# Attention on one Trainium2 core: every fourth score tile from bf16 parts, in the array shape of the value products, and a dealt copy of the keys

## The chip, the cores and the metric

The kernel runs on one core of a Trainium2 chip. The metric is device time of one execution, in microseconds (us). Engines are named as in the profile: PE (matmuls), PEld (PE's weight loads), DVE (vector), ACT (scalar), POOL (GpSimd), SP (the engine that issues most transfers).

## The reference

Two layers, each attention and a feed-forward part. The change concerns the attention of the first, over 4096 tokens of 256 features, 16 heads of 16:

```
q, k, v = split_heads(x @ Wq.T + bq), split_heads(x @ Wk.T + bk), split_heads(x @ Wv.T + bv)
scores = einsum('hbnd,hbmd->hbnm', k, q) / 16
attn   = softmax(scores, axis=-1)                 # over the 4096 m
out    = einsum('hbnm,hbmd->hbnd', attn, v)       # then @ Wo.T + bo
```

`x` is the normalised input. Everything is float32 at the interface.

## The kernel before, in words

The stages run one after the other: weights are turned (`setup_phase`), projections (`qkv0_phase`), attention (`attention_phase`), the first feed-forward part, and the second layer. Each engine runs its own program; waits are on semaphores counted.

**Projections.** Eight blocks of 512 tokens. PE makes queries and keys feature by feature, in four slices c = 0 to 3 of 128 features (0, 1 queries, 2, 3 keys). ACT writes the high part (fp32r) of each, DVE the low part (`low`, L450); SP stores both parts to the scratch tensors QS and KS (L348). DVE also writes the values into `V_all`. POOL does nothing.

**Attention.** Heads go in pairs, eight of them, and a pair's 4096 key positions in eight blocks of 512: 64 steps. `QST` holds the pair's queries and `KST` (four slots) the blocks' keys as stacks of 16-row parts (high, high, low against high, low, high), so that one matmul of 48 rows makes a product of split numbers. Head e of the pair has rows 64e and up, so the two heads' matmuls use different row halves of PE's array. For every block two kinds of product are made:

- A tiles (`unit_a`, L624): keys as weights, every fourth key for each of four groups, 512 queries streamed. DVE takes the maxima over queries (L719), one reduction of 128 x 1024 for the two heads of a pair of A tiles. After 32 of them `neg` (L726) is the negative maximum of every key; POOL cuts it into parts (L749, L751) and SP writes them as two more rows of `KST` (`load_shift`, L587).
- Score tiles (`unit_s`, L636): 128 queries as weights, 50 rows, 512 keys streamed, into one of three PSUM banks `SB`. ACT takes the exponential (L696) into `PR`. A score tile waits until ACT has read the bank's tile before it, three earlier (`s_free`).

The A tiles run one block ahead and LEAD = 8 chunks more. The values (`values`, L646) are products of 128 rows and 32 columns: four of them stand side by side in PE's array, each with its own 32 columns, one for each head and each of two chunks, accumulating over all chunks in one bank `PV` of 128 x 512. In fp32 each is two matmul instructions. PE's order per two chunks of 128 queries: score head 0, A pair, score head 1, the same again, then four values products. At a step's end ACT copies `PV` to `OS` (L707), POOL moves the odd chunks' groups beside the even ones by two transfers (L763), adds them (L766), and stores numerators and denominators (L773). Keys of a block are loaded by six transfers three steps ahead (L572), queries of the next pair by six at a pair's first step. Each engine's attention program is a loop whose body holds 16 steps, turned four times.

## Time and profile before

| | us |
|---|---|
| time, median of 3 runs | 5075.87 (5071.74 to 5075.96) |
| the profiled execution: its time | 5077.41 |
| its span in the profile | 5075.5 |
| PE busy in the span | 4705.6 |
| DVE busy | 3645.4 |
| ACT busy | 3173.7 |
| POOL busy | 394.2 |

The span is what the profile covers; the profiled execution took 1.9 us more than it, and 1.5 us more than the median. A busy PE is not PE at its peak: its matmuls are pipelined and overlap in the records, so the distance of their starts counts.

### The profile page before, as it was taken

The page shows a single profiled execution, that of the slowest core. Times are in us where ns is not written, and L with a number is a line of the kernel's source. Part 1 is how long each engine was busy: PE and PEld are TensorE (multiplying, and loading weights), DVE is VectorE, ACT ScalarE, POOL GpSimd, SP SyncE. Part 2 cuts the span into 40 slices and gives each one's busy share as a digit, 9 for nine tenths or more (in the row PEclk, how much of TensorE's full clock was granted, in tenths as well). Part 3 has the DMA queues.
Part 4 walks back from the last instruction along what each step waited for, and adds up shares of the span by engine and source line. Part 5 has one row for each costly group of instructions (what it writes and reads, how often), then busy time and mean ns, then how long its engine had stood idle before and what let it go on. Part 6 is the DMA issues. An engine that isn't in the chain of part 4 may idle for free. (4 is left out here: it accounts for less than half of the span.)

```text
span 5075.5 us, 80926 instructions
## 1 busy us (share of the span) xinstructions
PE 4705.6 (93%) x24956; PEld 2773.9 (55%) x24956; DVE 3645.4 (72%) x3695; ACT 3173.7 (63%) x5605; POOL 394.2 (8%) x866
## 2 busy tenths in 40 slices
PE   6699999999999999999999959999885399999999
PEld 4344444444444444444444437777654177777777
DVE  4789999899998999998999965565455444444444
ACT  3178778788887787787878744444473344444444
POOL 0001111111111111111111100000000000000000
PEclk8699999999999999999999979999997699999999
DMA  4310100100101001001010020000001400000000
GB/s 146 96 16 12 26 12 12 22 13 13 25 12 24 12 12 25 13 13 23 12 25 12 13 81 25 33 25 17 23 21 46 114 6 11 12 12 12 12 12 13
DMA packets 145888, 135.28 MB, mean 27 GB/s; under 512 B 83360, under 2 KB 102192, under 8 KB 144720
## 3 DMA queue, kind: packets, MB, share of 16 engines
q1 hardware_dynamic: 133296, 114.48, 9.1%
q0 software_dynamic: 12288, 16.80, 1.6%
q8 instruction: 185, 3.03, 0.3%
q14 instruction: 119, 0.97, 0.1%
HBM read 80.33 MB, written 41.94 MB: 24 GB/s over the span
## 5 line engine op out<-in xcount | busy, mean ns | idle before, releaser
L719 DVE TENSOR_REDUCE PM<-A 128x2 f32<-128x1024 f32 x2090 | 2460.9, 1221 | 292.9 <-PE A L624 292.9
L696 ACT ACTIVATE PR<-SB 128x512 f32<-128x512 f32 x4100 | 2118.2, 605 | 548.0 <-PE SB L636 539.7
L636 PE MATMUL SB<-KST,QST 50*128 50x512 f32 x4100 | 1508.6, 449 | 20.3 <-issue 8.4
L636 PEld LDWEIGHTS SB<-KST,QST 50*128 50x128 f32 x4100 | 699.9, 191 | 1186.7 <-ACT PR L696 1158.5
L624 PE MATMUL A<-QST,KST 48*128 48x512 f32 x4180 | 1273.1, 484 | 37.5 <-DMA QST<-QS 24.7
L646 PE MATMUL PV<-PR,VH 128*32 128x512 f32 x8192 | 1098.8, 609 | 0.0
L624 PEld LDWEIGHTS A<-QST,KST 48*128 48x128 f32 x4180 | 764.3, 306 | 106.9 <-DVE PM L719 43.0
L1860 DVE TENSOR_TENSOR m_h_lo<-m_h_full,m_h_hi 128x512 fp32r<-128x512 f32 x320 | 221.7, 693 | 285.3 <-ACT m_h_hi L1765 285.0
L1765 ACT CAST m_h_hi<-m_h_full 128x512 fp32r<-128x512 f32 x320 | 198.5, 620 | 245.5 <-DVE m_h_full L1857 243.4
L1857 DVE TENSOR_TENSOR m_h_full<-m_h_full,m_c 128x512 f32<-128x512 f32 x256 | 175.3, 685 | 235.2 <-ACT m_h_full L1759 204.8
L646 PEld LDWEIGHTS PV<-PR,VH 128*32 128x32 f32 x8192 | 161.5, 108 | 252.5 <-issue 163.4
L1759 ACT ACTIVATE m_h_full<-m_h,m_b 128x512 f32<-128x512 f32 x256 | 175.8, 687 | 195.1 <-PE m_h L58 194.4
L1071 DVE SCALAR_TENSOR_TENSOR chosen<-gate_out,h_ps 128x512 f32<-128x512 f32 x128 | 87.2, 681 | 181.1 <-PE h_ps L58 181.1
L1010 ACT ACTIVATE h_full<-chosen,b 128x512 f32<-128x512 f32 x128 | 92.4, 722 | 198.0 <-DVE chosen L1071 197.2
L56 PE MATMUL m_h<-ln_hi,moe_w_hi 128*128 128x512 f32 x512 | 208.7, 408 | 0.0
L57 PE MATMUL m_h<-ln_lo,moe_w_hi 128*128 128x512 f32 x512 | 202.8, 396 | 0.0
L56 PE MATMUL m_y<-m_h_hi,moe_w_hi 128*128 128x512 f32 x512 | 201.9, 394 | 0.0
L58 PE MATMUL m_h<-ln_hi,moe_w_lo 128*128 128x512 f32 x512 | 201.8, 394 | 0.0
L58 PE MATMUL m_y<-m_h_hi,moe_w_lo 128*128 128x512 f32 x512 | 201.5, 394 | 0.0
L57 PE MATMUL m_y<-m_h_lo,moe_w_hi 128*128 128x512 f32 x512 | 200.3, 391 | 0.0
L1080 DVE TENSOR_TENSOR h_lo<-h_full,h_hi 128x512 fp32r<-128x512 f32 x192 | 131.3, 684 | 71.6 <-ACT h_hi L1012 71.3
L1656 POOL CAST pick_pair<-pick 128x128 fp32r<-128x128 f32 x256 | 81.7, 319 | 1003.9 <-PE m_c L1678 1002.0
(283 smaller groups left out, 5187.4 us busy)
## 6 DMA issues: line engine op xcount, KB each, us to landing
QST<-QS SPq DMA_DIRECT2D x54, 256.0 KB, 8.4
KST<-KS SPq DMA_DIRECT2D x402, 32.0 KB, 1.8
QS<-parts SPq DMA_DIRECT2D x16, 512.0 KB, 2.8
KS<-parts SPq DMA_DIRECT2D x16, 512.0 KB, 2.8
OG<-OS POOLq DMA_DIRECT2D x128, 64.0 KB, 1.9
m_x<-X3T SPq DMA_DIRECT2D x16, 512.0 KB, 3.7
KST<-NM SPq DMA_DIRECT2D x260, 2.0 KB, 2.0
x_tok<-in_L_attn_x SPq DMA_DIRECT2D x8, 512.0 KB, 4.7
```

The lines of the kernel that those rows point to most:

```text
L56: nc.tensor.matmul(out, w[0], x[0], start=first, stop=False)
L57: nc.tensor.matmul(out, w[0], x[1], start=False, stop=False)
L58: return nc.tensor.matmul(out, w[1], x[0], start=False, stop=last)
L624: return nc.tensor.matmul(A[:, u % 2 * 2 + e, :], keys, QST[rows, slot, j * TB:(j + 1) * TB], start=True, stop=True)
L636: nc.tensor.matmul(SB[:, s_bank(v), :], QST[rows, slot, c * P:(c + 1) * P], KST[rows, nb % K_SLOTS, :], start=True, stop=True).then_inc(s_ ...
L646: mm = nc.tensor.matmul(PV[at:at + 2 * HD, :], VH[:, slot, e, c, :], PR[:, (2 * c + e) % P_SLOTS, :], start=(k == 0), stop=(k == PVS - 1))
L696: nc.scalar.activation(PR[:, v % P_SLOTS, :], SB[:, s_bank(v), :], ACT.Exp, scale=SCALE).then_inc(s_free, 1)
L719: nc.vector.tensor_reduce(PM[:, par, :, i, j:j + 1], A[:, u % 2 * 2:u % 2 * 2 + 2, :], AX.X, ALU.max).then_inc(a_free, 1)
L1759: nc.scalar.activation(h_full[:, c % RING, :], h_ps[:, c % 2, :], ACT.Silu, bias=bias).then_inc(full_ready, 1)
L1765: nc.scalar.copy(h[0][:, c % RING, :], h_full[:, c % RING, :]).then_inc(hi_ready, 1)
L1857: nc.vector.tensor_tensor(h_full[:, c % RING, :], h_full[:, c % RING, :], c_ps[:, c % 2, :], ALU.mult).then_inc(kept_ready, 1)
L1860: nc.vector.tensor_tensor(h[1][:, c % RING, :], h_full[:, c % RING, :], h[0][:, c % RING, :].bitcast(F32), ALU.subtract).then_inc(lo_ready, 1)
```

## The change

- Heads are paired (p, p + 8) in place of (2p, 2p + 1), so that head 1 of a pair lies in the features 128 and up.
- The score tile of head 1 and every odd chunk, one of four, is made by `unit_fine`: four matmuls of 99 rows and 32 columns, 512 keys streamed, side by side in the array. Its operands `QF` and `KF` are bf16, three parts of each number in six products of 16 rows, and three rows for the shift.
- The values are taken per chunk: four products, for two heads and two halves of 256 keys, into `PV[:, 0:256]`. `PV` then holds finished sums: POOL's two transfers and addition go, eight stores take their place. There are four values products more per two chunks, each of half the columns. The fine tile stands between the values of two chunks.
- PE's order per two chunks: A pair, score, score, score, A pair (its two halves in the other order), values, fine tile, values. LEAD is 10.
- A dealt copy of the keys, `KAD` in memory and `KA` on chip, holds each group of 128 keys of A's weights contiguously.
- The projections' new POOL program makes the dealt copy and the three bf16 parts of queries (features 128 and up, odd chunks) and keys; SP stores them after the block's other stores.
- Per block SP loads keys by 18 transfers in place of six, per pair queries by 12 in place of six, and the shift by seven in place of four.

```diff
@@ qkv0_phase, SP, per block
+                    for k in range(KC):
+                        sp.wait_ge(dealt_ready, count(((i + 2) * KC + (k + 1)) * PARTS))
+                        alone(sp, passed)
+                        sp.dma_start(d["KAD"].rearrange("j (k p) n -> p k j n", p=P)[:, k, :, ds(i, TB)],
+                                     dealt[slot][:, k, :, :].bitcast(F32)).then_inc(dealt_stored[slot], 16)
+                    for n, c in enumerate((1, 3)):
+                        sp.wait_ge(fine_ready, count(i * 2 * FINE + (n + 1) * FINE))
+                        alone(sp, passed)
+                        dst, cols = (d["QFD"], OB) if c == 1 else (d["KFD"], TB)
+                        sp.dma_start(dst.rearrange("j p n -> p j n")[:, :, ds(i, cols)],
+                                     fine[slot][c][:, :, :]).then_inc(fine_stored[slot], 16)
@@ qkv0_phase, POOL (new)
+                def fine_parts(half, i, slot, n, c):
...
+                    nc.gpsimd.tensor_tensor(of(whole), of(parts[slot][:, c, 0, :].bitcast(F32)),
+                                            of(parts[slot][:, c, 1, :].bitcast(F32)), ALU.add).then_inc(summed, 1)
...
+                    for j in range(FINE):
+                        nc.gpsimd.tensor_copy(part(j), of(left)).then_inc(fine_ready, 1)
+                        if j < FINE - 1:
+                            pool.wait_ge(fine_ready, count(k * FINE + (j + 1)))
+                            nc.gpsimd.tensor_tensor(of(rest[j]), of(left), part(j), ALU.subtract).then_inc(rest_ready, 1)
...
+                def deal(half, i, slot, c):
...
+                    for j in range(PARTS):
+                        nc.gpsimd.tensor_copy(dealt[slot][:, c - 2, j, :].bitcast(F32).rearrange("p (i q) -> p i q", i=TT),
+                                              parts[slot][:, c, j, :].bitcast(F32).rearrange("p (q i) -> p i q", i=TT)
+                                              ).then_inc(dealt_ready, 1)
+
+                def blocks(half, i, slot, following):
+                    fine_parts(half, i, slot, 0, 1)
+                    deal(half, i, slot, 2)
+                    deal(half, i, slot, 3)
+                    fine_parts(half, i, slot, 1, 3)
@@ attention_phase, SP
                 def load_k(pair, nb):
...
+                    load_stack(KA[:, nb % K_SLOTS, :], "KAD", K_PARTS, pair, cols, ready)
+                    load_stack(KST[:, nb % K_SLOTS, :], "KS", K_PARTS, pair, cols, ready)
+                    load_fine(KF[:, nb % K_SLOTS, :], "KFD", FINE_K, pair, cols, ready)
@@ load_shift
+                    sp.wait_ge(neg_fine, count((b + 1) * FINE))
+                    for j in range(FINE):
+                        row = FINE_STACK + j
+                        sp.dma_start(KF[row:row + 1, nb % K_SLOTS, :], NF[:, nb % 2, j, :], allow_slow_non_contiguous=True
+                                     ).then_inc(shift_loaded[nb % 2], 16)
@@ attention_phase, PE
-                    keys = KST[rows, nb % K_SLOTS, :].rearrange("r (p i) -> r i p", i=TT)[:, i, :]
+                    keys = KA[rows, nb % K_SLOTS, i * P:(i + 1) * P]
...
+                def unit_fine(t, c, nb, slot):
+                    v = 2 * c + 1
+                    pe.wait_ge(s_free, count(t * EXPS + (s_before(v) + 1 + S_BANKS)))
+                    for r in range(4):
+                        at = c // 2 * P + r * 2 * HD
+                        mm = nc.tensor.matmul(SB[r * 2 * HD:(r + 1) * 2 * HD, s_bank(v), :],
+                                              QF[0:FINE_ROWS, slot, at:at + 2 * HD],
+                                              KF[0:FINE_ROWS, nb % K_SLOTS, :], start=True, stop=True)
+                    mm.then_inc(s_done, 1)
+
+                def values(t, c, slot):
+                    if c == 0:
                         pe.wait_ge(pv_read, count(t))
...
+                    pe.wait_ge(s_free, count(t * EXPS + (2 * c + 2 + S_BANKS)))
+                    for e in range(2):
+                        for b in range(2):
+                            at = HALF * e + 2 * HD * b
+                            mm = nc.tensor.matmul(PV[at:at + 2 * HD, 0:HB], VH[:, slot, e, c, :],
+                                                  PR[:, (2 * c + e) % P_SLOTS, b * HB:(b + 1) * HB],
+                                                  start=(c == 0), stop=(c == MC - 1))
                     mm.then_inc(p_free, 1)
...
+                        units_a(t + ahead, u, a_nb, a_slot)
                         unit_s(s_t, q % MC, 0, s_nb, s_slot)
-                        units_a(t + ahead, u, a_nb, 1 - hp if past else hp)
                         unit_s(s_t, q % MC, 1, s_nb, s_slot)
...
+                        unit_s(s_t, q % MC + 1, 0, s_nb, s_slot)
+                        units_a(t + ahead, u + 1, a_nb, a_slot)
...
+                        values(t, q - 2, hp)
+                        unit_fine(s_t, q % MC + 1, s_nb, s_slot)
+                        values(t, q - 1, hp)
@@ attention_phase, ACT
-                    nc.scalar.copy(OS[:, nb % 2, :], PV[:, :]).then_inc(pv_read, 1)
+                    nc.scalar.copy(OS[:, nb % 2, :], PV[:, 0:HB]).then_inc(pv_read, 1)
@@ attention_phase, DVE, at the start
+                    nc.vector.memset(QF[:, s, :], 1.0).then_inc(rows_set, 1)
                     nc.vector.memset(QST[:, s, :].bitcast(F32), 1.0).then_inc(rows_set, 1)
@@ attention_phase, POOL, shift_parts
+                    left = neg[:, par, TT:2 * TT]
+                    for j in range(FINE):
...
+                        nc.gpsimd.tensor_copy(NF[:, par, j, :], left).then_inc(neg_fine, 1)
+                        if j < FINE - 1:
+                            pool.wait_ge(neg_fine, count(b * FINE + (j + 1)))
+                            nc.gpsimd.tensor_tensor(neg_rest[j][:, :], left, NF[:, par, j, :],
+                                                    ALU.subtract).then_inc(neg_left, 1)
...
@@ attention_phase, POOL, step
-                    for e in range(2):
-                        pool.dma_start(OG[HALF * e:HALF * e + 2 * HD, :],
-                                       OS[HALF * e + 2 * HD:HALF * (e + 1), nb % 2, :]).then_inc(groups_moved, 16)
-                    pool.wait_ge(groups_moved, (t + 1) * 32)
-                    nc.gpsimd.tensor_tensor(O2[0:P - 2 * HD, :], OS[0:P - 2 * HD, nb % 2, :], OG[0:P - 2 * HD, :],
-                                            ALU.add).then_inc(os_free, 1)
...
+                        for b in range(2):
+                            for j, name in enumerate(("NUM", "DEN")):
+                                at = HALF * e + 2 * HD * b + HD * j
+                                pool.dma_start(d[name][bass.ds(pair * HD + e * P, HD),
+                                                       nb * TB + b * HB:nb * TB + (b + 1) * HB],
+                                               OS[at:at + HD, nb % 2, :]).then_inc(o_stored, 16)
```

## Rows read from the trace of the kernel before

**Rows 1.** The page, busy time of each engine over the span.
```profile
PE 4705.6 (93%) x24956; PEld 2773.9 (55%) x24956; DVE 3645.4 (72%) x3695; ACT 3173.7 (63%) x5605; POOL 394.2 (8%) x866
```
**Rows 2.** ACT's copy by line: duration min/median/max in ns, first and last start in us.
```profile
L707 ACT COPY OS<-PV x64: 585/587/588, 296.2 to 2962.3; 128x512 f32<-128x512 f32 x64
```
**Rows 3.** Timeline of two periods: start, length (us), engine, line; idle before in brackets.
```profile
1504.88 0.50 PE L636 MATMUL SB<-KST,QST 50*128 50x512 f32 x1
...
1504.88 0.73 PE L624 MATMUL A<-QST,KST 48*128 48x512 f32 x2
...
1505.34 0.51 PE L636 MATMUL SB<-KST,QST 50*128 50x512 f32 x2
1505.41 2.06 ACT L696 ACTIVATE PR<-SB 128x512 f32<-128x512 f32 x4 [0.55 <-PE SB L636]
...
1505.56 0.51 PE L624 MATMUL A<-QST,KST 48*128 48x512 f32 x2
1505.64 2.36 DVE L719 TENSOR_REDUCE PM<-A 128x2 f32<-128x1024 f32 x2 [0.24 <-PE A L624]
1506.06 0.18 PEld L636 LDWEIGHTS SB<-KST,QST 50*128 50x128 f32 x1 [0.30 <-ACT PR L696]
1506.06 0.49 PE L636 MATMUL SB<-KST,QST 50*128 50x512 f32 x1
...
1506.48 1.06 PE L646 MATMUL PV<-PR,VH 128*32 128x512 f32 x8
...
1507.48 0.50 PE L636 MATMUL SB<-KST,QST 50*128 50x512 f32 x1
...
1508.04 0.22 DVE L726 TENSOR_REDUCE neg<-PM 128x8 f32<-128x64 f32 x1
1508.05 0.31 PEld L624 LDWEIGHTS A<-QST,KST 48*128 48x128 f32 x2
...
1508.91 1.77 SPq L587 DMA_DIRECT2D KST<-NM  x3
...
1510.09 0.50 PE L636 MATMUL SB<-KST,QST 50*128 50x512 f32 x1
```
**Rows 4.** Timeline of PE in the last stage, fp32 between fp32r matmuls.
```profile
4086.46 1.88 PE L130 MATMUL m_turn<-m_x,ones 128*128 128x512 f32 x4
...
4088.41 0.40 PE L57 MATMUL m_h<-ln_lo,moe_w_hi 128*128 128x512 f32 x1
4088.64 0.40 PE L58 MATMUL m_h<-ln_hi,moe_w_lo 128*128 128x512 f32 x1
```
**Rows 5.** PE's sequencer by line: the values' wait, and the loop's end.
```profile
L642 PEldq ALU_OP  x64: 32/32/32, 294.6 to 2960.6; - x64
...
L556 PEldq ALU_OP  x4: 32/32/32, 923.5 to 2960.8; - x4
...
L556 PEldq COMPARE_BRANCH  x4: 83/3856/4046, 923.7 to 2960.8; - x4
```
**Rows 6.** Timeline at the projections' end and attention's start, DVE and SP's queue.
```profile
176.90 0.75 DVE L450 SCALAR_TENSOR_TENSOR parts<-qk_ps,qk_bias,parts 128x512 fp32r<-128x512 f32 x1 [0.88 <-ACT parts L421]
...
183.87 2.67 SPq L572 DMA_DIRECT2D KST<-KS  x6
...
188.30 2.62 SPq L572 DMA_DIRECT2D QST<-QS  x6
```
**Rows 7.** One block of the projections: busy us of each engine, clock, DMA share, GB/s.
```profile
140.00:157.00 17.00, 14.02 (x69) 10.30 (x68) 11.63 (x12) 6.32 (x9) 0.00 (x0) 1.00 0.46 170
```
**Rows 8.** POOL's copy of the values by line.
```profile
L743 POOL COPY VH<-V_all x16: 609/612/617, 186.4 to 2302.0; 128x512 f32 x12, 128x512 f32<-128x512 f32 x4
```
**Rows 9.** A's weight loads by line.
```profile
L624 PEld LDWEIGHTS A<-QST,KST x4180: 304/306/338, 203.6 to 2960.0; 48*128 48x128 f32 x200
```
**Rows 10.** Timeline at attention's end, POOL.
```profile
2966.02 1.25 POOL L766 TENSOR_TENSOR O<-OS,OG 96x512 f32<-96x512 f32 x1 [1.51 <-DMA OG<-OS]
...
2972.39 0.48 POOL L773 DMA_DIRECT2D DEN<-O x1
```

More of the change, by code:

```diff
@@ L298 @@
 PARTS = 2
+FINE = 3
+OB = TB // 2
 def qkv0_phase(nc, d, K, V_all):
@@ L311, in qkv0_phase @@
         parts = [sb(f"parts{s}", [P, 4, PARTS, TB], F32R) for s in range(2)]
+        whole, rest = sb("whole", [P, TB], F32), [sb(f"rest{j}", [P, TB], F32) for j in range(2)]
+        fine = [{1: sb(f"fine_q{s}", [P, FINE, OB], BF16), 3: sb(f"fine_k{s}", [P, FINE, TB], BF16)} for s in range(2)]
+        dealt = [sb(f"dealt{s}", [P, KC, PARTS, TB], F32R) for s in range(2)]
         qk_bias = sb("qk_bias", [P, 4], F32)
@@ L321, in qkv0_phase @@
         qk_stored = [sem(f"qk_stored{s}") for s in range(2)]
+        fine_stored = [sem(f"fine_stored{s}") for s in range(2)]
+        summed, fine_ready, rest_ready, pool_passed = (sem(n) for n in ("summed", "fine_ready", "rest_ready", "pool_passed"))
+        dealt_ready, dealt_stored = sem("dealt_ready"), [sem(f"dealt_stored{s}") for s in range(2)]
         ln = LayerNorm("ln0", nc, sb, sem, K["ones"], [xT], xT_ready, ln_ps[:, 0, :], ln_ps[:, 1, :], 2)
@@ L444, in _, with of, part @@
                 overlapped(act, blocks)
+            @block.gpsimd
+            def _(pool):
+                def fine_parts(half, i, slot, n, c):
+                    def of(t):
+                        if c == 3:
+                            return t[:, :]
+                        return t[:, :].rearrange("p (a b m) -> p a b m", a=2, b=2)[:, :, 1, :]
+                    def part(j):
+                        return fine[slot][c][:, j, :] if c == 3 else fine[slot][c][:, j, :].rearrange(
+                            "p (a m) -> p a m", a=2)
+                    k = i * 2 + n
+                    pool.wait_ge(low_ready, count(i * 4 + (c + 1)))
+                    pool.wait_ge(fine_stored[slot], count(half * 32))
+                    pool.wait_ge(fine_ready, count(k * FINE))
+                    alone(pool, pool_passed)
+                    nc.gpsimd.tensor_tensor(of(whole), of(parts[slot][:, c, 0, :].bitcast(F32)),
+                                            of(parts[slot][:, c, 1, :].bitcast(F32)), ALU.add).then_inc(summed, 1)
+                    pool.wait_ge(summed, count(k + 1 + 4))
+                    alone(pool, pool_passed)
+                    left = whole
+                    for j in range(FINE):
[3 more added lines that the diff above has]
+                            nc.gpsimd.tensor_tensor(of(rest[j]), of(left), part(j), ALU.subtract).then_inc(rest_ready, 1)
+                            pool.wait_ge(rest_ready, count(k * (FINE - 1) + (j + 1)))
+                            alone(pool, pool_passed)
+                            left = rest[j]
+                def deal(half, i, slot, c):
+                    pool.wait_ge(low_ready, count(i * 4 + (c + 1)))
+                    pool.wait_ge(dealt_stored[slot], count(half * 32))
+                    alone(pool, pool_passed)
+                    for j in range(PARTS):
[7 more added lines that the diff above has]
+                    fine_parts(half, i, slot, 1, 3)
+                pool.sem_inc(summed, 4)
+                pool.sem_inc(dealt_ready, 2 * KC * PARTS)
+                overlapped(pool, blocks)
@@ L495 @@
 ROWS = STACK + PARTS
+FINE_K = (0, 0, 1, 0, 1, 2)
+FINE_Q = (0, 1, 0, 2, 1, 0)
+FINE_STACK = len(FINE_K) * HD
+FINE_ROWS = FINE_STACK + FINE
 HALF = P // 2
 SCALE = 1.0 / D ** 0.5
-LEAD = 8
+LEAD = 10
 EXPS = 2 * MC
-PVS = MC // 2
+HB = TB // 2
 S_BANKS = 3
@@ L534, in attention_phase @@
         NM = sb("NM", [P, 2, PARTS, 2 * TT], F32R)
-        OS = sb("OS", [P, 2, TB], F32)
-        OG = sb("OG", [P, TB], F32)
-        O2 = sb("O2", [P, TB], F32)
+        KA = sb("KA", [P, K_SLOTS, TB], F32R)
+        QF = sb("QF", [P, 2, T // 2], BF16)
+        KF = sb("KF", [P, K_SLOTS, TB], BF16)
+        NF = sb("NF", [P, 2, FINE, TT], BF16)
+        neg_rest = [sb(f"neg_rest{j}", [P, TT], F32) for j in range(FINE - 1)]
+        OS = sb("OS", [P, 2, HB], F32)
         A = ps("A", [P, 4, TB])
@@ L628, in units_a @@
                     pe.wait_ge(a_free, count(b * MC + (u + 1)))
-                    unit_a(u, 1, nb, slot)
-                    unit_a(u, 0, nb, slot).then_inc(a_done, 1)
+                    first = u % 2
+                    unit_a(u, first, nb, slot)
+                    unit_a(u, 1 - first, nb, slot).then_inc(a_done, 1)
                 def unit_s(t, c, e, nb, slot):
@@ L651, in step @@
                     t = number(two, hp, nb)
-                    for q in range(2, MC + 2):
+                    for q in range(2, MC + 2, 2):
                         ahead, u = divmod(q + LEAD, MC)
@@ L683, in _ @@
                 pe.wait_ge(shift_loaded[0], count(SHIFT))
-                for q in range(2):
-                    unit_s(0, q, 0, 0, 0)
-                    units_a(1, q + LEAD, 1, 0)
-                    unit_s(0, q, 1, 0, 0)
+                units_a(1, LEAD, 1, 0)
+                unit_s(0, 0, 0, 0, 0)
+                unit_s(0, 0, 1, 0, 0)
+                unit_s(0, 1, 0, 0, 0)
+                units_a(1, LEAD + 1, 1, 0)
+                unit_fine(0, 1, 0, 0)
                 in_steps(pe, step)
```

87 lines of the change are left out of this document (45 added, 42 removed).

## The prediction

> **What bounds the kernel.** I read the page first: PE 93%, DVE 72%, ACT 63% busy [rows 1]. Those are averages over five stages. The copy of the accumulated values happens once a step, 64 times from 296.2 to 2962.3 us [rows 2], so the attention stage is 63 steps in 2666.1 us, 42.32 us each, or 53% of the span. All of the change lies in it and in the projection stage before it.
>
> Next the timeline of one period, which is two chunks of 128 queries, sixteen to a step [rows 3]. The period is the distance of equal rows: 1504.88 to 1510.09 is two, so 2.605 us. The reader should see three things.
>
> *First*, PE's period has two sections. In the "stack" section (1504.88 to 1506.48, 1.60 us) four score tiles and two pairs of A tiles go, in the two row halves of the array, each half a queue of 512-column matmuls. In the values section (1506.48 to 1507.48, 1.00 us) eight matmul instructions go, four side by side, in two rounds.
>
> *Second*, the stack section holds a wait. Its first seven matmuls start at 1504.88 to about 1505.68 (the pair at 1505.56 ends at 1506.07 and each is 0.40 long). The last score tile starts only at 1506.06: its weight load stood 0.30 us behind ACT. That is the three-bank limit: tile 3 reuses the bank of tile 0, whose exponential starts at 1505.41 and takes 0.60. That row half had last started a matmul at 1505.56 and could have taken the next 0.23 later, so about 0.27 us of each period is PE waiting for an exponential.
>
> *Third*, the others have slack, but not much. ACT does its four in 2.06 and idles 0.55. DVE does its two reductions in 2.36 and idles 0.24, and the second A pair's weights (1508.05) come 0.05 after DVE's second reduction (1505.64 + 2.36 = 1508.00). So DVE stands right behind PE.
>
> **The stack section after.** One of four score tiles leaves, and it is the one that waited. Both row halves are now queues of four (A, score, score, A) and three. A half's queue advances by 0.23: in [rows 3] the tiles of one half start at 1504.88, 1505.22, 1505.45 and about 1505.68 (the first step also holds its exposed weight load, 0.10, which is 0.50 against 0.40 of duration). The last start is then at 0.81. From the last score's start to the values' start is 1506.48 - 1506.06 = 0.42; less its exposed weight load 0.10 it is 0.32. So the section is 0.81 + 0.32 = 1.13, 0.47 less than 1.60. The contiguous keys shorten the A weight load from 0.31 to at best the 0.18 of the score's [rows 3]; these loads lie beside running matmuls, so I give this nothing here (at best 0.1).
>
> **The values section after.** Before: two rounds, starting 1506.48 and 1506.95 (the group ends at 1507.54, a matmul of the second round is 0.59), so 0.46 a round. A 512-column fp32 matmul advances PE by 0.43 (four in 1.88 with 0.59 for the last [rows 4]), so a round costs 0.43 + 0.03, and the change of shape at the end 1.00 - 0.92 = 0.08. After: the same values work in four rounds of 256 columns, each 0.215 + 0.03 = 0.245, and one round for the fine tile, four bf16 matmuls of 512 columns. No bf16 matmul stands in the trace. Bounds for its round: 0.23, the spacing of single-pass matmuls [rows 4], and 0.46, the fp32 round of this shape. I take 0.25, since only its dtype is new and one pass of 512 columns has the former's length. Going from fp32 to another type costs nothing seen: the fp32 group's last start is 4087.75, and the second matmul behind it starts at 4088.41, which is 0.43 + 0.23 [rows 4]. Sum: 4 x 0.245 + 0.25 + 0.08 = 1.31.
>
> PE alone would then take 1.13 + 1.31 = 2.44, or 2.30 without the rounds' surplus over their columns.
>
> The rule that weighs against this change is in the Trainium skill, "TensorEngine Tiling (Array Packing)", Instruction Overhead: each matmul carries about 60 cycles. At 2.4 GHz that is 25 ns, as an estimate. By it the 20 instructions of the new values section cost 0.50 over their columns and the period is 2.30 + 0.50 = 2.80. The trace disagrees: the eight instructions of today's section cost 0.06 over their columns, not 0.20 [rows 3]; carried over by instruction that is 0.15, by round 0.14.
>
> Nor is the issuing of instructions the limit: between the values' wait (2960.6) and the loop's end (2960.8) PE's sequencer passes 16 instructions in 0.2 us [rows 5], and a period will have 54.
>
> **DVE's loop.** The first reduction can start when the first A pair is done. That pair now leads the section: 0.50 with an exposed load, 0.11 for the load of the second, 0.04 until DVE starts, 0.65 (before: 0.76, 1505.64 - 1504.88). Two reductions take 2.36, and the second A pair may load 0.05 later, at 3.06 from the start. It wants to load at 0.57 of the next period (1508.05 - 1507.48). If it comes x later, the section is x longer: P = 2.44 + x and P + 0.57 + x = 3.06, so x = 0.025 and P = 2.465. With PE at its lower bound (half rounds without the 0.03 and the fine round at 0.23: 2.30) the same two lines give 2.395. ACT, at four exponentials 0.49 apart, is hidden, and the fine tile's bank is free in time: exponential 0 ends near 1.36, the fine tile starts near 1.65.
>
> Saved: 2.605 - 2.465 = 0.14. Of 1024 periods I leave out 13, at the stage's start and after the three turns of its loop, where PE's branch takes 3.86 us [rows 5] and more code does not change that: 1011 x 0.14 = **-142 us**.
>
> **Once per step.** ACT's copy (0.59 [rows 2]) is halved and gets out of the exponentials' way; DVE's `neg` reduction (0.22), which fitted in the idle 0.24, loses part of its cover. I take 0 for both, bounds +-0.2 x 64 = +-13. POOL gets five more small operations (short like `neg`, 0.22, and as much waiting) and SP three more transfers (0.6 each, 1.77 for three [rows 3]) before the shift is in place: with two reductions, `neg` and seven transfers about 9 us, and the landing of the last. With LEAD 10 there are six periods, 14.7 us, from the block's last A pair to the next step's first score; with 8 there were five, 12.3, so it would be just enough. SP's 18 key loads per step at 0.45 each (six in 2.67 [rows 6]) are 8 us of 39, and at a pair's start 12 query loads add 5: both are hidden by the step.
>
> **Projection stage.** POOL was idle in it, and a block takes 17 us with the DMA engines 46% busy [rows 7]. Now POOL does, per block: three tensor-tensors of 512 and three of 256 columns, casts likewise, four dealing copies. From 1.25 for a tensor-tensor of 512 columns and 0.61 for a copy of 512 [rows 8, 10]: 3 x 1.25 + 3 x 0.73 + (4 + 3) x 0.61 + 3 x 0.4 + waits 1.5 = 13 us. That is under 17, so it is hidden except at the end: the last keys' part is ready at 177.65 [rows 6]; POOL then has about 10 us left, plus the store, where before only the store followed. **+10**. Collisions with DVE: none at best, at worst each of 16 large DVE operations behind a 1.25 operation, 20 us; I take **+5**. The Trainium skill, "SBUF — State Buffer", SBUF: two separate sides, has a VectorE operation with two SBUF inputs and a GpSimd operation that reads SBUF shut each other out for their whole length; by it the sum would have up to +20 there. No row shows it.
>
> **Start and end of attention.** SP's first keys are 18 loads, not 6: +5.3, of which 4.4 were spent waiting for the memset (183.87 to 188.30 [rows 6]), so the queries go out about 3.7 later; they are 12 transfers with a quarter more bytes, over the 13 us to the first A at 203.6 [rows 9]: +4. Two more A pairs before the first score: +2.3. Together **+10**. At the end the transfer of groups and the addition go: the stores ran from 2966.02 + 1.25 to 2972.9, now eight issues of 0.49 start at once [rows 10]: **-5**.
>
> **Sum:** -142 + 0 + 10 + 5 + 10 - 5 = -122. The profiled execution is 5077.4 us; the median 5075.9 is 1.5 lower. 5075.9 - 122 = **4954**.
>
> **Rivals.**
> *PE shorter (chance 0.27).* The shorter weight loads and cheap half rounds help, and DVE's loop decides: P = 2.395, -212, time 4884. For it: 0.31 against 0.18 of weight load. Against: those loads are covered.
> *A new wait in the loop (0.12).* The fine tile's exponential comes last and the next section's third score wants its bank; a period of 2.55: 1011 x 0.055 = -56, time 5040. For it: the chain before was one of this kind. Against: I find 0.2 us of slack.
> *POOL bounds the projection (0.08).* Strided dealing or collisions stretch 13 us over 17, say to 21: 8 x 4 = +32, time 4986.
> *Slower (0.06, and 0.01 for 25 ns on each of the 20 instructions, +0.195 x 1011 = +197, time 5250).* The four fine matmuls do not run side by side but one after the other, 0.92 instead of 0.25: P = 3.11, +510, time 5600. It decides from a fine round of 0.39 on (P 2.605). For it: four streams of the same rows in a new type are not in the trace. Against: fp32 ones run side by side.
> *The forecast (0.46).*
>
> So faster by over 0.2% (10 us, what a measurement here can tell) 0.92, within it 0.01, slower 0.07. The range holds the forecast, the first and third rivals and their bounds: 4865 to 5020.
>
> **What would show it.** Right: equal rows 2.40 to 2.50 apart; no weight load of a score behind ACT for 0.3; DVE with almost no idle; a values section near 1.3 with five rounds. Wrong: fine matmuls that start 0.23 apart; a section above 1.5; DVE idle while the period is above 2.5; the first A much after 225.

## The result, and the profile after the change

The changed kernel takes 4906.1 us (median of 4 runs, 4899.7 to 4913.5) where the kernel before takes 5075.9 (4 runs, 5071.7 to 5083.0): a ratio of 0.9665, with a 95% interval of 0.9647 to 0.9682. So it is 3.3% faster. The forecast was 4954 (4865 to 5020): the sign and the range are right, but the saving is 170 us and not 122. The profiled execution of the changed kernel took 4904.4, its span is 4902.7, against a span of 5075.5 before.

The page of the changed kernel, busy time of each engine, against [rows 1]:
```profile
PE 4503.7 (92%) x36227; PEld 2730.8 (56%) x36227; DVE 3647.4 (74%) x3699; ACT 3162.0 (64%) x5605; POOL 538.8 (11%) x1382
```
PE is busy for 202 us less, with 11271 more instructions. DVE and ACT do the same work as before.

**Where the 172.8 us of the span went.** Five marks cut it. The first and the last exponential stand in ACT's line (duration min/median/max in ns, then first and last start in us), of the changed kernel and then of the one before:
```profile
L814 ACT ACTIVATE PR<-SB x4100: 591/598/620, 284.6 to 2782.1; 128x512 f32<-128x512 f32 x196
```
```profile
L696 ACT ACTIVATE PR<-SB x4100: 592/606/633, 250.5 to 2961.4; 128x512 f32<-128x512 f32 x196
```
| stretch | before | after | difference | forecast |
|---|---|---|---|---|
| start to attention's first load (183.87, 208.34) | 183.9 | 208.3 | +24.5 | +15 |
| to the first exponential | 66.6 | 76.3 | +9.6 | +10 |
| first to last exponential | 2710.9 | 2497.5 | -213.4 | -142 |
| to the next stage's first load (2978.88, 2803.48) | 17.4 | 21.4 | +4.0 | -5 |
| the rest | 2096.6 | 2099.2 | +2.6 | 0 |

**The period.** The timeline of two periods of the changed kernel (start, length, engine, line), against [rows 3]:
```profile
1505.39 0.50 PE L724 MATMUL A<-QST,KA 48*128 48x512 f32 x2
...
1505.72 0.64 PE L737 MATMUL SB<-KST,QST 50*128 50x512 f32 x3
1505.86 0.18 PEld L737 LDWEIGHTS SB<-KST,QST 50*128 50x128 f32 x1 [0.18 <-ACT PR L814]
...
1505.95 0.65 PE L724 MATMUL A<-QST,KA 48*128 48x512 f32 x2
1506.15 2.06 ACT L814 ACTIVATE PR<-SB 128x512 f32<-128x512 f32 x4 [0.34 <-PE SB L737]
...
1506.54 0.64 PE L757 MATMUL PV<-PR,VH 128*32 128x256 f32 x8
...
1506.99 0.40 PE L745 MATMUL SB<-KF,QF 99*32 99x512 bf16 x4
...
1507.21 0.61 PE L757 MATMUL PV<-PR,VH 128*32 128x256 f32 x8
...
1507.76 0.49 PE L724 MATMUL A<-QST,KA 48*128 48x512 f32 x2
...
1510.16 0.49 PE L724 MATMUL A<-QST,KA 48*128 48x512 f32 x2
```
From 1505.39 to 1510.16 is two periods: 2.385 us each, where before had 2.605. The stack section (1505.39 to 1506.54) takes 1.15, the values section (1506.54 to 1507.76) 1.22. In the latter the first two rounds take 0.45, the fine tile's round 0.22, the last two with the change of shape 0.55. The only wait named is that of the third score's weights, 0.18 behind ACT. Over the whole stage the distance of the first exponentials of two steps has a median of 41.90 us before and 38.43 after, sixteen periods in each: 2.619 and 2.402.

**The end of the projections.** The last low part, POOL's work behind it, and attention's first load, against [rows 6]:
```profile
190.51 0.75 DVE L528 SCALAR_TENSOR_TENSOR parts<-qk_ps,qk_bias,parts 128x512 fp32r<-128x512 f32 x1 [1.09 <-ACT parts L448]
...
192.28 4.17 POOL L510 COPY dealt<-parts 128x512 f32<-128x512 f32 x4
...
196.41 1.26 POOL L491 TENSOR_TENSOR whole<-parts 128x512 f32<-128x512 f32 x1
...
201.86 0.61 POOL L497 CAST fine_k<-rest 128x512 bf16<-128x512 f32 x1 [0.17 <-POOL rest L500]
202.55 0.37 SPq L368 DMA_DIRECT2D KFD<-fine_k  x1
208.34 2.68 SPq L659 DMA_DIRECT2D KA<-KAD  x6
```
The last keys' low part is ready at 191.26, where it was ready at 177.65: 13.6 of the 24.5 us are lost before POOL's tail, and 10.9 in it.

One block of the projections after, beside [rows 7]: POOL is busy for 12.38 of 17 us, DMA 0.76.
```profile
140.00:157.00 17.00, 12.84 (x49) 8.34 (x47) 10.08 (x11) 6.23 (x8) 12.38 (x15) 0.90 0.76 275
```
The clock of a single block tells little: it is 0.90 here against 1.00 in [rows 7], but before the change it is 0.90 in the block ahead of that too (123 to 140 us). Over the whole stretch up to the last low part it is 0.95 before and 0.89 after:
```profile
52.00:178.00 126.00, 103.76 (x475) 76.15 (x474) 81.17 (x82) 44.78 (x58) 0.00 (x0) 0.95 0.49 174
```
```profile
52.00:191.00 139.00, 110.40 (x470) 79.19 (x470) 86.57 (x81) 45.45 (x59) 99.69 (x116) 0.89 0.65 232
```

### The profile page after: what moved, and what is told of

Read it like the earlier page. It is cut to its first block and busy times, and to the rows that moved or that the text cites. A ratio compares the mean times of both kernels' runs of the same rounds, so it can differ in the third digit from the quotient of the medians.

```text
span 4902.7 us, 107872 instructions
## 1 busy us (share of the span) xinstructions
PE 4503.7 (92%) x36227; PEld 2730.8 (56%) x36227; DVE 3647.4 (74%) x3699; ACT 3162.0 (64%) x5605; POOL 538.8 (11%) x1382
## 5 line engine op out<-in xcount | busy, mean ns | idle before, releaser
L757 PE MATMUL PV<-PR,VH 128*32 128x256 f32 x16384 | 1292.5, 386 | 2.4 <-issue 2.4
L724 PE MATMUL A<-QST,KA 48*128 48x512 f32 x4184 | 1193.2, 475 | 66.8 <-DMA QF<-QFD 41.7
L757 PEld LDWEIGHTS PV<-PR,VH 128*32 128x32 f32 x16384 | 432.9, 110 | 555.3 <-issue 367.8
L724 PEld LDWEIGHTS A<-QST,KA 48*128 48x128 f32 x4184 | 426.7, 187 | 524.0 <-issue 454.6
L737 PE MATMUL SB<-KST,QST 50*128 50x512 f32 x3075 | 687.6, 411 | 0.2
L737 PEld LDWEIGHTS SB<-KST,QST 50*128 50x128 f32 x3075 | 386.6, 186 | 207.8 <-ACT PR L814 204.8
L745 PE MATMUL SB<-KF,QF 99*32 99x512 bf16 x4100 | 415.7, 384 | 5.5 <-issue 4.3
L896 POOL DMA_DIRECT2D NUM<-OS x256 | 126.6, 494 | 864.2 <-ACT OS L825 721.0
```

Source lines behind the costliest of these rows:

```text
L724: return nc.tensor.matmul(A[:, u % 2 * 2 + e, :], keys, QST[rows, slot, j * TB:(j + 1) * TB], start=True, stop=True)
L737: nc.tensor.matmul(SB[:, s_bank(v), :], QST[rows, slot, c * P:(c + 1) * P], KST[rows, nb % K_SLOTS, :], start=True, stop=True).then_inc(s_ ...
L745: mm = nc.tensor.matmul(SB[r * 2 * HD:(r + 1) * 2 * HD, s_bank(v), :], QF[0:FINE_ROWS, slot, at:at + 2 * HD], KF[0:FINE_ROWS, nb % K_SLOTS ...
L757: mm = nc.tensor.matmul(PV[at:at + 2 * HD, 0:HB], VH[:, slot, e, c, :], PR[:, (2 * c + e) % P_SLOTS, b * HB:(b + 1) * HB], start=(c == 0), ...
```

## The experiments

Each is the changed kernel with one edit; the last has two together. Where no number of runs is given, the time is that of one run. The changed kernel's own runs lie within 14 us, so a difference of a few us in a single time tells nothing; such differences are read from the trace.

### The fine round between, ahead of or behind the values

The working had priced the fine tile at 0.25 and found 0.2 us of slack for its exponential. Moving its round tells whether PE or a chain through ACT sets the period.
```
-                        values(t, q - 2, hp)
                         unit_fine(s_t, q % MC + 1, s_nb, s_slot)
+                        values(t, q - 2, hp)
                         values(t, q - 1, hp)
```


> The fine tile stands ahead of both chunks' values, not between them; all else is as after the change. Theory (PE's two sections add up, and the fine tile is placed where its bank is free): it now waits for the exponential of the section's first score, which ends 1.36 us into the period where the values section begins at 1.15, so the period grows from 2.39 by about 0.25 to 2.63 and the time to about 5155. Rival (DVE's chain of reductions sets the period, the place of the tile is indifferent): period 2.39, time 4906.

Measured: 5111.6 us, periods 2.61 apart (the kernel before beside it: 5072.3). The timeline, weights and matmuls of the fine tile:
```profile
1505.54 0.10 PEld L745 LDWEIGHTS SB<-KF,QF 99*32 99x32 bf16 x4 [0.66 <-ACT PR L814]
1505.54 0.40 PE L745 MATMUL SB<-KF,QF 99*32 99x512 bf16 x4 [0.21 <-ACT PR L814]
```
The tile now waits for the exponential of the first score, which holds its bank, as the fourth score did in [rows 3]. The whole saving is gone: the same four matmuls are worth the saving only where a bank is free.
```
                         values(t, q - 2, hp)
-                        unit_fine(s_t, q % MC + 1, s_nb, s_slot)
                         values(t, q - 1, hp)
+                        unit_fine(s_t, q % MC + 1, s_nb, s_slot)
```


> The fine tile stands behind both chunks' values. Theory: its result is 0.43 us later, so its exponential ends about 3.05 after the period's start, and the third score of the next stack section waits for that bank: from 2.35 + x = P and P + 0.57 + x = 3.23 the period is 2.50, time about 5020, with a weight load of a score waiting about 0.3 us behind ACT. Rival (DVE's chain sets the period): 2.39, 4906.

Measured: 5146.6 us, periods 2.64 apart. This was a miss: I had reckoned 2.50. What is late is the *next* section's third score:
```profile
1505.98 0.18 PEld L737 LDWEIGHTS SB<-KST,QST 50*128 50x128 f32 x1 [0.46 <-ACT PR L814]
```
It wants the bank that the fine tile's exponential frees. In the changed kernel the same row shows 0.18 of waiting; here the fine round begins 0.33 before the section's end (1504.89 against 1505.22), its exponential at 1505.33. My figure had left out that the loop closes: when the section grows, the fine round moves back with it. So the middle place is the only one of the three that pays, and it is not free of ACT either (0.18).

### The tile back in the stack section, on the new kernel

```
                         unit_s(s_t, q % MC + 1, 0, s_nb, s_slot)
+                        unit_s(s_t, q % MC + 1, 1, s_nb, s_slot)
...
-                        unit_fine(s_t, q % MC + 1, s_nb, s_slot)
```


> The fourth score tile is made as before the change, one matmul of 50 rows in the stack section, last in it; everything else (order, values by chunk, dealt keys, projections) is as after. Theory (the gain is the fourth tile's place): the tile waits for exponential 0, which now ends 1.36 us into the period, starts at 1.41, the values section begins at 1.84 and lasts 1.00, so the period is 2.84 and the time about 5365, slower than before the change. Rival (order, dealt keys and values by chunk carry a share of the gain by themselves): period 2.6 or less, at most 5130.

Measured: 5348.7 us, periods 2.85 apart. With A leading the section and four half rounds, but the score in its old shape, the last score's weights wait for ACT, and the values stand behind them:
```profile
1507.11 0.18 PEld L737 LDWEIGHTS SB<-KST,QST 50*128 50x128 f32 x1 [0.66 <-ACT PR L814]
1507.11 0.50 PE L737 MATMUL SB<-KST,QST 50*128 50x512 f32 x1 [0.21 <-ACT PR L814]
1507.54 0.57 PEld L757 LDWEIGHTS PV<-PR,VH 128*32 128x32 f32 x13 [0.25 <-ACT PR L814]
```
(The prologue's one fine tile goes back too.) That is 0.47 us more than with the fine tile. So there is no gain without the tile's move: the order, the half rounds and the dealt keys without it make the kernel slower than before.

### The price of a fine round, and of the keys' layout

```
-                    for r in range(4):
+                    for r in range(8):
+                        r %= 4
```


> The fine tile is made twice (eight matmuls into the same bank, same result). Theory: one more round of 0.216 us in the values section; the 0.04 that PE loses to ACT and DVE is absorbed, so the period is 2.39 + 0.17 to 0.22, time 5080 to 5130. Rival (DVE sets the period and PE has slack): less than 0.05 more, under 4960.

Measured: 5085.0 us, periods 2.57 apart, 0.18 more. The eight matmuls and the next values:
```profile
1506.77 0.62 PE L746 MATMUL SB<-KF,QF 99*32 99x512 bf16 x8
...
1507.21 0.62 PE L758 MATMUL PV<-PR,VH 128*32 128x256 f32 x8
```
Two rounds take 0.44, so one takes 0.22: four bf16 matmuls of 512 columns do run side by side at the pace of one. That the period grows by less (0.18) is the wait behind ACT, which is used up.
```
-                    keys = KA[rows, nb % K_SLOTS, i * P:(i + 1) * P]
+                    keys = KST[rows, nb % K_SLOTS, :].rearrange("r (p i) -> r i p", i=TT)[:, i, :]
```


> The A tiles take their weights from the score keys with a stride of four, as before the change; the dealt copy is still made and loaded. Theory: the weight load grows from 0.18 to 0.31 us, and both pairs show it, the first because it opens the section, the second because it may only start when DVE's second reduction has ended: period 2.39 + 0.12 to 0.24, time 5030 to 5150. Rival (the prediction's: these loads lie beside running matmuls): 2.39, 4906.

Measured: 4996.0 us, periods 2.48 apart, 0.09 more, below the 0.12 to 0.24 expected (the second copy is still made and loaded).
```profile
1504.72 0.31 PEld L724 LDWEIGHTS A<-QST,KST 48*128 48x128 f32 x2 [0.41 <-issue]
1504.72 0.62 PE L724 MATMUL A<-QST,KST 48*128 48x512 f32 x2
```
The pair that leads the section is 0.62 long and not 0.50, since its load (0.31 and not 0.19) lies bare at the change of shape. So reading A's weights from the dealt copy is worth 90 us, with the fine tile in place; what making the copy costs in the projections is not in this number, and it is no share of the 170 that adds to the tile's own, since tile_in_stack loses over 440 us with the copy in place. I had given this 0, "at best 0.1": it is near the upper bound.

### Is DVE the bound of the loop?

This kernel reduces only half of A's columns, so each key's maximum is taken over half of the queries.
```
-                    nc.vector.tensor_reduce(PM[:, par, :, i, j:j + 1], A[:, u % 2 * 2:u % 2 * 2 + 2, :], AX.X,
+                    nc.vector.tensor_reduce(PM[:, par, :, i, j:j + 1], A[:, u % 2 * 2:u % 2 * 2 + 2, 0:TB // 2], AX.X,
```


> DVE takes the maxima over half of the columns only, so each reduction is about 0.7 us in place of 1.22; the maxima are then not the true ones. Theory: DVE costs the period only the 0.01 to 0.03 by which the second A pair's weights wait for it, so the period goes from 2.387 to 2.36 to 2.38 and the time to 4880 to 4900. Rival (DVE's chain sets the period): PE's own 2.30 or less, time under 4840.

Measured: 4882.0 us, but from the first to the last exponential 2494.4 against 2497.5, with the same period of 2.39. In the steady stretch from 300 to 850 us, the changed kernel, then this one (busy us of PE, PEld, DVE, ACT, POOL, clock, DMA share, GB/s):
```profile
300.00:850.00 550.00, 548.73 (x6156) 260.02 (x6152) 537.92 (x471) 474.86 (x926) 74.06 (x212) 1.00 0.12 22
```
```profile
300.00:850.00 550.00, 549.09 (x6178) 259.33 (x6171) 319.63 (x473) 475.78 (x929) 75.34 (x219) 1.00 0.12 22
```
DVE falls from 538 to 320 us and PE stays full. So the loop is at PE's length, with the third score's wait behind ACT in it, and DVE, busy for 98% of it, stands right behind without lengthening it. Of the 22 us by which the span is shorter, 15 came at the start, where DVE's reductions are the chain: the first exponential is at 269.2 and not 284.6.

### POOL in the projections

POOL's operations there are cut to an eighth of their columns; the rest of the dealt keys and bf16 parts is zero, set once.
```
-                            return t[:, :]
+                            return t[:, 0:TB // 8]
...
-                        nc.gpsimd.tensor_copy(dealt[slot][:, c - 2, j, :].bitcast(F32).rearrange("p (i q) -> p i q", i=TT),
+                        nc.gpsimd.tensor_copy(dealt[slot][:, c - 2, j, 0:TB // 8].bitcast(F32),
```


> In the projections POOL works on an eighth of the columns of each operation (the rest of the bf16 parts and of the dealt keys stays zero, so scores and maxima are not the true ones); the stores keep their size. Theory: the start of attention, first key load at 208.3 us against 183.9 before the change, is late by POOL's tail behind the last keys and by its collisions with DVE's operations; both shrink and the first key load comes at 184 to 190, time 4882 to 4888. Rival (the added stores, about 1.6 MB a block, hold the projections up): first key load still after 200.

Measured: 4883.4 us, attention's first load at 189.44 instead of 208.34, the exponentials' stretch unchanged at 2497.6. The last low part is ready at 178.65 (before 177.65), and POOL's tail with the store takes the rest. DVE's two large operations of the projections, after and in this kernel (count, busy us, mean ns, idle before):
```profile
L163 DVE TENSOR_TENSOR ln_lo<-ln_xc,ln_hi 128x1024 fp32r<-128x1024 f32 x8 | 14.7, 1834 | 4.3 <-ACT ln_hi L177 4.3
L157 DVE TENSOR_TENSOR ln_xc<-ln_xc,ln_sq 128x1024 f32<-128x1024 f32 x8 | 10.7, 1340 | 0.3
```
```profile
L163 DVE TENSOR_TENSOR ln_lo<-ln_xc,ln_hi 128x1024 fp32r<-128x1024 f32 x8 | 9.9, 1234 | 4.3 <-ACT ln_hi L177 4.3
L157 DVE TENSOR_TENSOR ln_xc<-ln_xc,ln_sq 128x1024 f32<-128x1024 f32 x8 | 9.8, 1226 | 0.3
```
18.9 of the 24.5 us go with POOL's columns: about 12.6 ahead of the last low part (13.6 less the 1.0 left here), the rest in the tail. POOL's width lengthens DVE's operations by 4.8 + 0.9 = 5.7 us in all. By the Trainium skill, "SBUF — State Buffer", SBUF: two separate sides, a VectorE operation with two SBUF inputs and a GpSimd operation that reads SBUF shut each other out, and the one that starts first keeps the other waiting for its whole length. The trace agrees. This is one block of the changed kernel:
```profile
160.65 1.10 POOL L510 COPY dealt<-parts 128x512 f32<-128x512 f32 x1 [2.10 <-DVE parts L528]
160.91 1.93 DVE L163 TENSOR_TENSOR ln_lo<-ln_xc,ln_hi 128x1024 fp32r<-128x1024 f32 x1 [0.45 <-ACT ln_hi L177]
161.68 2.14 POOL L510 COPY dealt<-parts 128x512 f32<-128x512 f32 x1
```
L163 starts 0.26 behind a dealing copy and ends 1.09 behind that copy's end, which leaves room for most of its own 1.22; the next copy takes 2.14 where their median is 1.12, and ends 0.98 behind L163. So it is in all seven blocks with a successor (1.91 to 1.93). It goes the other way in light_pool: there POOL's add of 64 columns starts 0.11 behind L163 and takes 1.30 in each of the seven, against 0.33 the one time that no L163 runs, and L163 keeps its 1.23.

The remaining 7 us of the 12.6 have no single row. No row has PE, ACT or DVE waiting for POOL there, though ACT's new program has such waits. SyncE's queue does wait for it ahead of the new stores, and ACT waits longer for PE's products. The clock up to the last low part is 0.89 in the changed kernel and 0.94 here:
```profile
52.00:179.00 127.00, 104.11 (x476) 76.19 (x475) 81.47 (x82) 45.34 (x59) 35.41 (x121) 0.94 0.75 263
```
As an estimate from these rows, 0.11 x 139 less 0.06 x 127 is 7.7 us of PE at its upper level. That would be enough, but no run parts the clock from the waits.

### The stores and the order of the first loads

```
                     load_shift(t + 1, (nb + 1) % NB)
+                    sp.wait_ge(pv_read, count(t + 1))
...
+                                sp.dma_start(d[name][bass.ds(pair * HD + e * P, HD),
...
-                    pool.wait_ge(pv_read, count(t + 1))
...
-                                pool.dma_start(d[name][bass.ds(pair * HD + e * P, HD),
```


> The eight stores of each step go out on SP's queue, behind the shift's transfers, instead of POOL's. Theory: the 10.5 us for which POOL drains at the stage's end belong to its own transfers and go; the period is unchanged; time about 4896. Rival (the drain has another cause): it stays, time 4906 or, if SP's queue makes the key loads late, more.

Measured: 4895.5 us. GpSimd's drain at the stage's end starts once its last eight stores have landed. Here it is in the changed kernel, in the one before, and in this one (duration in ns, start in us):
```profile
L652 POOLq DRAIN  x1: 10515/10515/10515, 2788.7 to 2788.7; - x1
```
```profile
L565 POOLq DRAIN  x1: 552/552/552, 2974.4 to 2974.4; - x1
```
```profile
L652 POOLq DRAIN  x1: 34/34/34, 2791.5 to 2791.5; - x1
```
In the changed kernel the stores have landed by 2788.7, 6.6 us behind the last exponential (before: 13.0), and the next stage's first load stands 14.8 us further on, 10.5 of which are the drain. With SyncE's stores that load is at 2795.51, 9.7 behind the last exponential (2785.8) and not 21.4. The drain is 10.515 us long in each of the nine kernels here whose GpSimd issues these eight stores.
```
-                load_k(0, 0)
+                load_stack(KA[:, 0, :], "KAD", K_PARTS, 0, slice(0, TB), first_a)
+                sp.wait_ge(rows_set, count(1))
+                load_stack(QST[:, 0, :], "QS", Q_PARTS, 0, slice(0, T), first_a)
...
-                load_q(0, 0)
+                load_stack(KST[:, 0, :], "KS", K_PARTS, 0, slice(0, TB), k_loaded[0])
...
+                pe.wait_ge(first_a, count(16 * 4 * len(K_PARTS)))
```


> Edit: at the start VectorE clears the queries' tile first, SyncE loads the first values-shaped keys, then the first queries, and only then the coarse keys and the fine ones, and TensorE's first A waits for the first two alone. Theory (the start of attention is a chain: last load, first A, DVE's reductions of the prologue, first exponential): the first A comes as many loads earlier as now stand ahead of it, three of about 2 us each, so the first reduction at about 229 us instead of 235.2, the first exponential 5 to 6 us earlier (279 instead of 284.6), the period 2.39 as before, and the time about 4900. Rival (the DMA transfers bound the start, whatever their order): first reduction at 233 or later and the time within 2 us of the changed kernel's 4906.

Measured: 4886.4 us. The first reduction starts 20.6 us behind the first load, as in the kernel before, where the changed kernel needs 26.8; the first exponential is at 277.7, 6.9 earlier:
```profile
207.60 2.68 SPq L660 DMA_DIRECT2D KA<-KAD  x6
...
212.04 2.62 SPq L660 DMA_DIRECT2D QST<-QS  x6
...
228.25 12.53 DVE L845 TENSOR_REDUCE PM<-A 128x2 f32<-128x1024 f32 x11 [7.68 <-PE A L731]
```
That is better than the 4900 expected, and only 6.9 of it is the edit's: of the 17.9 us by which the span is shorter, 9.4 lie between the first and the last exponential, most of them behind the turns of the loops.

Both edits together:

> Edit: the changed kernel with the other order of the first loads and with attention's stores issued by SyncE instead of GpSimd. Theory (the drain of GpSimd behind attention, 10.5 us of which about 10 lay on the path, and the loads ahead of the first A are terms of their own): their gains add, some 10 us from the stores and 5 to 6 from the start, so 4888 to 4892 us, a ratio to before of 0.963 to 0.964, with a period of 2.39. Rival (the earlier start only moves waiting to the keys of the second chunk, or SyncE's stores hold up the later loads of keys): 4895 or more.

Measured, in five runs, below the 4888 to 4892 expected: 4872.7 us (4869.6 to 4879.1), beside 5078.4 of the kernel before (9 runs on that chip): 0.9598, interval 0.9584 to 0.9611. So the version with both edits beats both kernels, the changed one by the ratio of the ratios, 0.9598 / 0.9665 = 0.993, some 34 us. Of these 6.8 lie ahead of the first exponential, 12.4 behind the last, and 15.6 between, where I had expected nothing.

**Where the 15.6 lie.** From the starts of all exponentials: the periods are the same (38.45 a step against 38.43). What differs are the three steps behind a turn of the loops, which last longer than a median step by 4.6, 10.3 and 9.2 us in the changed kernel, and by 4.4, 4.4 and 3.6 in this one (before: 8.7, 8.7 and 7.5), together 11.8. In the changed kernel the second of them holds this:
```profile
1550.56 0.39 PE L745 MATMUL SB<-KF,QF 99*32 99x512 bf16 x2
1553.89 0.10 PEld L745 LDWEIGHTS SB<-KF,QF 99*32 99x32 bf16 x2 [3.43 <-issue]
1553.90 0.39 PE L745 MATMUL SB<-KF,QF 99*32 99x512 bf16 x2 [2.95 <-issue]
```
PE stops in the middle of a round of four, for 3.3 us, at a place with no wait in the program; the last two of the round's weight loads come as late as its matmuls. Three stretches around it:
```profile
1540.00:1545.00 5.00, 5.00 (x59) 2.44 (x56) 4.94 (x5) 4.17 (x9) 0.78 (x2) 1.00 0.97 116
1545.00:1550.00 5.00, 5.00 (x57) 2.25 (x54) 4.95 (x5) 4.37 (x9) 0.00 (x0) 1.00 0.90 107
1550.00:1560.00 10.00, 7.05 (x64) 3.11 (x66) 5.19 (x5) 4.73 (x10) 0.00 (x0) 0.83 0.28 42
```
It comes behind 10 us in which the DMA engines are 0.90 to 0.97 busy with the queries of the next pair, in a loop's first pass over its code. Code that arrives late would look like this, and the trace's record of single DMA packets bears it out. The queue q8, whose kind is "instruction", brings 273 packets of 16 KB in the run, in this loop 10.0 us apart in the median. Behind this turn they come at 1532.7 and then at 1550.7, 18.0 us apart across the stretch of busy DMA engines. The second takes 1.7 us, so it has landed at 1552.4, and PE goes on 1.5 us later. In the changed kernel six distances are over 14 us (18.0 to 19.4), each beside the loads of a pair's queries; the two that lie close behind a turn are the two at which PE stops (the other is 18.6, with a stop of 1.33 at 2180.3). The stores alone (4895.5) have 20.4 and 20.5 ahead of their two stops (2.28 and 2.54). In the version with both edits no distance is over 16.6, and PE has no idle stretch over 1.2 us but the turns'. No run moves the loads of the queries, so this cause is read and not tried.

The clock goes the same way. In the three steps it is at its lower level for 24 us in the changed kernel, for 37 with the stores alone (excess 11.7, 11.7 and 8.4), and for 7 in this one. As an estimate at half speed, 17 us less of it are 8.5 us, which with the stops' 4.3 roughly makes up the 11.8. Why the packets and the clock went better here is open.

So of the 34 us, 19 are explained by the two edits, 12 by turns that went better, and nearly 4 are spread over the other steps.

## Why the prediction was right, and where not

**What bounded the kernel.** Right. The exposed weight load behind ACT (0.30 in [rows 3]) was the thing to remove, and tile_in_stack and fine_first bring both the wait and the time back.

**The stack section** (1.13 in the working, 1.15 measured). Right to 0.02; the 0.02 is the third score's wait for ACT, 0.18 of it shown, mostly beside running matmuls (in fine_twice the wait is gone and the section takes 1.13). It is the small form of the second rival ("the next section's third score wants its bank"), whose mechanism is real: fine_last makes it 0.46 and the period 2.64.

**The values section** (1.31, measured 1.22). This is the step that failed, a term mis-sized. I gave every round its columns plus 0.03, from 0.46 for each of two rounds in [rows 3]. The 1506.95 behind that figure is the start of the second round's last matmul; its first starts at 1506.93, so the rounds are 0.45 apart and the second takes less. The 0.03 belongs to the first round of the section alone: the rounds after are 0.22 apart, of 256 fp32 columns or 512 bf16 ones alike. And the change of shape is 0.11 and not 0.08. So 0.45 + 0.22 + 0.55 instead of 5 surpluses. Before, the section's length gave no hint, because 0.46 + 0.46 + 0.08 and 0.46 + 0.43 + 0.11 are the same 1.00. 20 instructions take 1.22, and their columns alone (5 x 0.215) 1.08. The Trainium skill, "TensorEngine Tiling (Array Packing)", Instruction Overhead, has some 60 cycles for each; the 0.50 over the columns that the prediction estimated from it is not seen, with 0.14 measured.

**DVE's loop** (x = 0.025, a period of 2.465). Wrong as a term: with the section at 1.22 the two sections come to 2.37, and half_reduction shows that relieving DVE by 40% gives nothing. Right as a warning: DVE is busy for 98% of the stretch. The period that came (2.385) is that of the first rival (PE shorter, 2.395 and 4884), for its reason of cheap half rounds, and its chance of 0.27 was set too low; only its bound was another, for DVE doesn't decide. The total differs from its 4884 by the projections and the end.

**The total.** It came nearer than its terms did. By the table the attention stretch saved 71 us more than forecast, and the others lost 21 us more than forecast; that the two partly cancel was luck. One rival's price is also off by a sum: +197 with the 20 forecast for the other stages is 5293, and not 5250.

**From the period to the stage.** 1011 x (2.605 - 2.385) = 222; measured over the whole stage, 213. The turns are as long as before (25.0 and 24.1 us of excess in all); the 9 us lie in the other steps, which exceed the median step by 12 us in all where they exceeded it by 3.

**The keys' second copy.** I gave the shorter loads nothing, because they "lie beside running matmuls". That holds for the second pair. The first pair stands at the change of shape, where the load is bare, and strided_keys prices it at 0.09 a period. It was in the 0.50 "with an exposed load" of the working, which was taken from a load of 0.18: the number was right, and the sentence beside it wrong.

**Projections** (+15, measured +24.5). The tail was right (+10, measured +10.9). The collisions (+5) were right for DVE's own operations (5.7), but the stretch ahead of the tail lost 13.6. Of that, 5.7 are these collisions, 1.0 stays with light POOL, and 7 go with POOL's columns with the lower clock beside them, for a cause that stays open. The third rival (POOL bounds the projection) is not what happened, as POOL is busy for 12.4 of 17 us and no row has PE, ACT or DVE waiting for it.

**Start of attention** (+10, measured +9.6). Right in sum; of it 6.2 lie ahead of the first reduction (8 forecast) and 3.4 in the prologue (2.3).

**End of attention** (-5, measured +4.0). The step that I priced is right: the stores land 6.4 us sooner behind the last exponential. What failed is that nothing else was priced: GpSimd's drain takes 10.5 us where it took 0.55. Before, six transfers of its own stood ahead of it (two moves, four stores), now eight stores; stores_by_sp shows that they are its cause, and why six cost next to nothing stays open.

**Slower, by fine matmuls in series** (0.06). Refuted by the 0.22 of the fine round and its doubling.

## What to carry to other kernels

A work item that waits for a buffer's reader is worth moving to where the buffer is free anyway; but work the neighbouring places out as a closed loop, since the item moves with the period that it sets (behind both chunks' values in place of between them made it 0.25 us longer here). Where a section's length is to be carried to another mix of instructions, take entry, steady round and exit from separate rows: one average of two rounds mis-sized the saving by 0.09 a period, where the whole period was missed by 0.08. And look which weight load stands first behind a change of shape: it was the only one whose length counted here.

## What the runs showed of the hardware

- **Four bf16 matmuls of 32 columns of weights side by side** take 0.22 us a round of 512 columns, and a change from fp32 to bf16 and back between rounds costs nothing that the starts show.
- **A weight load with a stride of 16 bytes between its elements** takes 0.31 us and the contiguous one 0.19, for the same 48x128 tile.
- **GpSimd's drain** at a stage's end took 10.5 us behind eight of its own transfers that had landed (nine kernels), and 0.034 where SyncE had issued them.
- **VectorE and GpSimd shut each other out** in the projections: VectorE's operation of 1.22 us took up to 1.93 behind a dealing copy, the copy behind it 2.14 and not 1.12, and an add of 64 columns 1.30 and not 0.33.
- **PE can stop for 3 us with nothing to wait for**, in a loop's first pass with the DMA engines over 0.9 busy: the packet of instructions that starts as it stops came 18 us behind the last one, where 10 is usual. The clock then is below its upper level for some us: 0.83 over the ten around this stop, and 0.50 (the lower level of 1.2 GHz) in this stretch behind the loop's turn, before which PE had been busy for 2.29 of 5 us:
```profile
1527.00:1532.00 5.00, 2.29 (x27) 0.95 (x27) 2.70 (x3) 2.61 (x6) 1.24 (x3) 0.91 0.22 56
1532.00:1536.00 4.00, 3.88 (x27) 1.96 (x27) 2.45 (x2) 1.91 (x4) 2.67 (x6) 0.50 0.39 82
```
